# Phases of small matmuls placed next to each other in an attention kernel

## The chip, the core and the metric

The kernel runs on one core of one Trainium2 chip. The core has TensorE (PE in the profile; its weight loads are PEld), VectorE (DVE), ScalarE (ACT), GpSimd (POOL) and SyncE (SP), whose queue issues most DMAs. The metric is the device time of one execution in microseconds: 3090.34 us is the median of three runs (3089.7 to 3090.7).

## What is computed

The input is 8 images of 16 channels and 56 x 56 pixels. A convolution with nine 9 x 9 filters turns each image into 160 channels a pixel. Then come two transformer blocks with attention inside windows of 7 x 7 pixels, five heads of 32; the second block shifts the windows by three pixels and masks. A linear layer, a convolution back and a 1 x 1 convolution end it. Each block is:

```python
x = _ln(x, ln1g, ln1b)                       # over the 160 channels
qkv = _win_part(x) @ qkvw + qkvb
q, k, v = heads(...)                         # 49 positions, 5 heads, 32 wide
attn = softmax(q @ k.T * HEAD_DIM ** (-0.5) + bias (+ mask))
x = sc + _win_rev(attn @ v) @ projw + projb
x = x + gelu(_ln(x, ln2g, ln2b) @ w1 + b1) @ w2 + b2
```

## The kernel before

Three parts run one after the other: `phase_a` (first convolution and preparation of the weights, to about 170 us), `phase_b` (both blocks, to about 2890 us) and `phase_c` (the closing convolutions). The change is in `phase_b`.

`phase_b` works on strips of 14 rows of one image, 32 strips a layer, 64 in all. A function `body(i, la, lm, ln)` is written once for each engine, and `bodies` calls it for i from -1 to 64. A call mixes three strips: the attention of strip i (layer `la`), the MLP of strip i - 1 (layer `lm`), and the front part of strip i + 1 (layer `ln`: first norm, its turned copies, the products Q, K, V and B, where B holds the fifth head). Calls 1 to 32 have `lm` = 0, calls 33 to 63 have `lm` = 1; calls 2 to 30 and 34 to 62 run in loops. In this text a strip is one call of `body`, and it belongs to layer 0 or layer 1 by its `lm`. The MLP of layer 1 has one output tile more between the turn of z1 and Q0 (`mlp_out(2)`) and ends in four products `linear` with the closing linear layer.

The order of work on each engine is the order of the calls in its `body`; engines wait for each other on semaphores only. A wait holds all that stands behind it on its engine.

The attention of a strip has four groups of windows, j = 0 to 3. For each:

- `scores(j)` on TensorE writes q k into the first 245 columns of both PSUM banks of `so` (L1489); 20 products of 64 x 49, recorded as 40 matmuls. They wait for `s_sadd` (VectorE has read the scores before) and for `s_od` (VectorE has read earlier outputs), then comes a `nop`.
- `scores_biased(j)` on VectorE adds the bias into `sc` (L1248) and raises `s_sadd`; `scores_less_max(j)` takes the maximum (L1255) and subtracts it (L1258); `exps(j)` on ScalarE (L1089).
- `weights_turned(j)` on TensorE transposes the weights into `pt_ps` (L1498), `weights_out(j)` on ScalarE copies them to `pt` (L1094).
- `outputs(j)` on TensorE multiplies them by v into the columns from 256 of the same banks of `so` (L1510), again 40 recorded matmuls. `outputs(j)` on VectorE divides by the sum: a reciprocal (L1265) and two products into `os_` (L1268, L1272); it raises `s_od`.
- `outputs_turned(j)` on TensorE transposes `os_` (L1522); `outputs_hi(j)` on ScalarE (L1101) and `outputs_lo(j)` on VectorE (L1297) take it out in two parts.

Both kinds of small matmul use two row groups and two column groups of the array at once; row group r writes bank r of `so`. TensorE writes `so` only while VectorE does not read it, since both halves lie in the same banks.

Around them: `front_turned(hf)` on TensorE transposes z1 (L1430), which GpSimd completes (`repeat_rest`, L987); `front_hi(hf)` on ScalarE (L1053) and `front_lo(hf)` on VectorE (two operations, L1231) take it out; `front_product("Q", 0)` waits until the second operation of `front_lo(1)` is done. At the end of a strip `projection(n)` feeds the residual on VectorE (L1386), the statistics (L1182 to L1201), GpSimd's power (L1029), the second norm (L1205) and GpSimd's repeat of z2 (L987); then `mlp_turned(i, 0)` transposes z2 (L1430), and the next call's first `mlp_in` follows. `linear_out` on VectorE (L1286) takes out the linear products.

The time is set around the change by these lines on TensorE:

```python
reach(pe, s_od, n * NG + {0: 0, 1: 0, 2: 0, 3: 1}[j])      # scores(j, n), L1478
pe.wait_ge(s_sadd, i * NG + (3 if j == 0 else 4))           # outputs(j), L1504
if use == "Q0":
    pe.wait_ge(*a_freed(i, "T1C1"))                         # front_lo(1) is done
```

Of the kernel before, what the change touches and what calls it, by code (L numbers as in the profile page):

```python
# [45 lines left out]
NG = W // (2 * WIN)  # L46
# [660 lines left out]
def phase_b(nc, keep, late, xs0, xs1, ys):  # L707
    with ExitStack() as ctx:
# [333 lines left out]
        def _(act):  # L1042
            act_ = nc.scalar.activation

            def body(i, la, lm, ln):
# [91 lines left out]
                if la is not None:  # L1137
                    weights_out(0)
                    exps(2)
                if ln is not None:  # L1140
                    front_hi(1)
                if la is not None:
                    weights_out(1)
                    outputs_hi(0)
                if ln is not None:
                    queries(0)
                if la is not None:
                    weights_out(2)
                if ln is not None:
                    keys(0)  # L1150
                if la is not None:
                    outputs_hi(1)
                    exps(3)
# [23 lines left out]
        def _(dve):  # L1177
# [43 lines left out]
            def body(i, la, lm, ln):  # L1221
# [39 lines left out]
                def outputs(j):  # L1261

                    n = i * NG + j + 1
                    dve.wait_ge(s_of, n)
                    v.reciprocal(view(rd, 0, QP, 0, [[HEADS, 2], [1, HEADS]]),  # L1265
                                 view(so, 0, QP, OC + HD, [[512, 2], [VW, HEADS]])).then_inc(s_rec, 1)
# [81 lines left out]
                if lm is not None:  # L1348
                    mlp_out(0)
                if la is not None:  # L1350
                    scores_biased(2, i, la)
                    scores_less_max(2, i)
                if ln is not None:
# [3 lines left out]
                if la is not None:  # L1357
                    outputs(0)
                if ln is not None:
                    front_lo(1)  # L1360
                if lm == 1:
                    mlp_out(2)
                if la is not None:
                    scores_biased(3, i, la)
                    outputs_lo(0)
                    outputs(1)
                    scores_less_max(3, i)
                    outputs_lo(1)
                    outputs(2)
                    outputs(3)  # L1370
                    outputs_lo(2)
# [48 lines left out]
        def _(pe):  # L1420
# [12 lines left out]
            def body(i, la, lm, ln):  # L1433
# [38 lines left out]
                def scores(j, n):  # L1472
# [4 lines left out]
                    reach(pe, s_sadd, n * NG + j)  # L1477
                    reach(pe, s_od, n * NG + {0: 0, 1: 0, 2: 0, 3: 1}[j])  # L1478
                    pe.nop(nofuse=True)
# [21 lines left out]
                def outputs(j):  # L1501
                    pe.wait_ge(s_pte, i * NG + j + 1)
                    pe.wait_ge(*a_freed(i - 1, f"V{j}"))
                    pe.wait_ge(s_sadd, i * NG + (3 if j == 0 else 4))  # L1504
                    reach(pe, s_od, i * NG + j)
# [79 lines left out]
                if lm is not None:  # L1585
                    mlp_out(0)
                if la is not None:
                    scores(2, i)
                if ln is not None:
# [5 lines left out]
                if la is not None:  # L1595
                    outputs(0)
                if ln is not None:
                    front_turned(1)
# [6 lines left out]
                if la is not None:  # L1605
                    outputs_turned(0)
                    scores(3, i)
                if ln is not None:
                    front_product("Q", 0)
                if la is not None:  # L1610
                    outputs(1)
                    weights_turned(2)
                if ln is not None:
                    front_product("K", 0)
                if la is not None:
                    outputs_turned(1)
                if ln is not None:
# [13 lines left out]
                if la is not None:  # L1631
                    outputs(3)
                if lm is not None:
                    mlp_out(2 + lm)
# [14 lines left out]
                if ln is not None:  # L1649
                    values(2)  # L1650
                    scores(0, i + 1)
                if lm == 0:
# [321 lines left out]
```

## Time and profile before

| | |
|---|---|
| median of three runs | 3090.34 us |
| the profiled execution, first to last instruction | 3089.1 us |
| TensorE busy | 2989.3 us, 97% |
| weight loads busy | 2698.0 us, 87% |
| VectorE busy | 2223.4 us, 72% |
| ScalarE busy | 1715.3 us, 56% |
| GpSimd busy | 827.8 us, 27% |
| one strip, layer 0 / layer 1 | 40.86 / 44.37 us |

How to read the rows: times are microseconds from the start of the span. In a timeline a row is one instruction or several alike merged (x40), with its start, the time to the end of the last, the engine, the line of the kernel, and what is written from what. Brackets at the end hold the idle time of the engine before it and what ended it; "issue" means that nothing in the profile shows as the releaser. The ends of matmuls are modelled and overlap the next start, so the time between starts is what counts. A wait row gives the waiting engine, its tile and line, what it waited for, total, number of times and longest. In the list of windows, PEclk is the granted clock of TensorE as a share of its full 2.4 GHz.

### The profile page before, as it was taken

How to read it: one execution, taken by the hardware profiler on the slowest of the kernel's cores; microseconds unless marked ns; L12 is line 12 of the kernel's file. 1: busy time of each engine (PE TensorE's matmuls, PEld its weight loads, DVE VectorE, ACT ScalarE, POOL GpSimd, SP SyncE). 2: the span in 40 equal slices, each digit the busy share in tenths (PEclk: the TensorE clock that was granted, in tenths of full speed). 3: DMA queues.
4: the chain of work that ended last, by engine and by line, in shares of the span. 5: the costliest groups of instructions: out<-in, count | busy, mean ns of one | idle time of the engine just before them, and what ended most of it. 6: DMA issues, size and time to landing. Idle time of an engine off the chain costs nothing. (4 is left out here: it accounts for less than half of the span.)

```text
span 3089.1 us, 102841 instructions
## 1 busy us (share of the span) xinstructions
PE 2989.3 (97%) x39898; PEld 2698.0 (87%) x39898; DVE 2223.4 (72%) x6736; ACT 1715.3 (56%) x4076; POOL 827.8 (27%) x1470
## 2 busy tenths in 40 slices
PE   8889999999999999999999999999999999999799
PEld 6679888898888888898888888888888889888699
DVE  5667777777777777777777777777777777777422
ACT  6456656666655656666555655565556555655321
POOL 8122222222222222222232233223322332232110
PEclk9989999999999999999999999999999999999899
DMA  6411111111111111113111111111111111112284
GB/s 142 155 60 41 38 34 39 30 35 39 39 39 39 39 33 39 31 34 93 44 39 29 33 40 33 29 37 40 33 26 40 40 33 26 40 40 42 43 141 82
DMA packets 210425, 147.29 MB, mean 48 GB/s; under 512 B 15955, under 2 KB 205206, under 8 KB 210332
## 3 DMA queue, kind: packets, MB, share of 16 engines
q1 hardware_dynamic: 207619, 142.41, 19.7%
q10 hardware_dynamic: 1008, 3.44, 0.5%
q0 software_dynamic: 1728, 0.48, 0.1%
q8 instruction: 48, 0.79, 0.1%
q14 instruction: 22, 0.17, 0.0%
HBM read 95.64 MB, written 52.50 MB: 48 GB/s over the span
## 5 line engine op out<-in xcount | busy, mean ns | idle before, releaser
L1543 PE MATMUL rm<-w,ht 128*112 128x160 f32 x4480 | 682.7, 302 | 0.0
L1543 PEld LDWEIGHTS rm<-w,ht 128*112 128x112 f32 x4480 | 611.8, 177 | 5.2
L1029 POOL TENSOR_TENSOR rs<-ln_tmp,mhalf 112x4 f32<-112x4 f32 (+1 forms) x128 | 119.1, 931 | 1625.0 <-DVE ln_tmp L1201 1624.9
L1119 ACT ACTIVATE ht<-rm 128x448 f32<-128x448 f32 (+1 forms) x640 | 319.0, 498 | 193.4 <-PE rm L127 193.4
L1084 ACT ACTIVATE vb<-ra 113x320 f32<-113x320 f32 x256 | 113.1, 442 | 278.4 <-PE ra L127 276.8
L127 PE MATMUL rm<-z2t_hi,w_hi 128*128 128x448 f32 (+1 forms) x640 | 257.2, 402 | 4.4 <-DVE z2t_rest L1309 3.3
L987 POOL TENSOR_TENSOR z<-z,one 112x448 f32<-112x448 f32 (+2 forms) x192 | 131.3, 684 | 354.9 <-DVE z L1205 354.9
L127 PE MATMUL rm<-z2t_rest,w_rest 98*128 98x448 f32 (+1 forms) x640 | 219.9, 344 | 0.0
L127 PE MATMUL rm<-z2t_lo,w_hi 128*128 128x448 f32 (+1 forms) x640 | 219.1, 342 | 0.0
L127 PE MATMUL rm<-z2t_hi,w_lo 128*128 128x448 f32 (+1 forms) x640 | 218.2, 341 | 0.0
L1248 DVE TENSOR_TENSOR sc<-so,tabs 113x490 f32<-113x490 f32 x256 | 171.3, 669 | 54.8 <-PE so L1489 42.5
L1510 PEld LDWEIGHTS so<-vb,pt 49*49 49x49 f32 x10240 | 142.6, 122 | 60.3 <-issue 55.0
L1265 DVE RECIPROCAL rd<-so 113x10 f32<-113x10 f32 x256 | 56.1, 219 | 190.7 <-PE so L1510 183.0
L1101 ACT ACTIVATE ot_hi<-ra 128x98 fp32r<-128x98 f32 x512 | 103.1, 260 | 152.5 <-PE ra L1522 151.0
L127 PEld LDWEIGHTS rm<-z2t_hi,w_hi 128*128 128x128 f32 x640 | 121.0, 189 | 73.5 <-ACT ht L1119 37.1
L1258 DVE TENSOR_TENSOR sm<-sc,mx 113x490 f32<-113x490 f32 x256 | 173.1, 676 | 13.9
L1489 PEld LDWEIGHTS so<-kt,qm 64*49 64x49 f32 x8192 | 140.9, 122 | 48.0 <-issue 42.6
L1430 PE MATMUL ra<-ident,z 112*128 112x112 f32 (+1 forms) x1280 | 164.3, 268 | 14.8 <-POOL z L987 13.8
L1060 ACT ACTIVATE qm<-ra,qpair 128x400 f32<-128x400 f32 x256 | 138.2, 591 | 69.9 <-PE ra L127 69.9
L1255 DVE TENSOR_REDUCE mx<-sc 113x10 f32<-113x490 f32 x256 | 169.2, 661 | 6.4
L1489 PE MATMUL so<-kt,qm 64*49 64x49 f32 x8192 | 172.7, 208 | 1.0 <-ACT k L1076 1.0
L1510 PE MATMUL so<-vb,pt 49*49 49x33 f32 x10240 | 170.0, 210 | 2.9 <-issue 0.9
(258 smaller groups left out, 8848.5 us busy)
## 6 DMA issues: line engine op xcount, KB each, us to landing
xa<-xs SPq DMA_DIRECT2D x128, 245.0 KB
xr<-xs SPq DMA_DIRECT2D x128, 245.0 KB
xs<-xo SPq DMA_DIRECT2D x64, 245.0 KB
ys<-yz SPq DMA_DIRECT2D x64, 245.0 KB
c_y<-ys SPq DMA_DIRECT2D x36, 260.0 KB
xs<-a_tok SPq DMA_DIRECT2D x14, 560.0 KB, 6.6
xs<-tok_late SPq DMA_DIRECT2D x14, 560.0 KB, 6.8
a_nat<-in_x ACTq DMA_DIRECT2D x7, 480.0 KB, 6.4
```

What stands on the lines that cost most here:

```text
L127: last = nc.tensor.matmul(out, lhs, rhs, start=(n == 0), stop=(n == len(pairs) - 1))
L987: gp.tensor_tensor(view(t, 0, TT, t0 * ZW + DIM, [[ZW, nt], [REST, 2], [1, REST]]), once, view(one, 0, TT, 0, [[0, nt], [0, 2], [0, REST]] ...
L1029: gp.tensor_tensor(rs[1][:, t0:t0 + nt], ln_tmp[1][5][:, t0:t0 + nt], mhalf[:, 0:nt], ALU.pow).then_inc(s_pow, 1)
L1060: last = act_(qm[:, odd * QN + hf * QH:odd * QN + (hf + 1) * QH], bank_a(i, use)[:, 0:QH], ACT.Copy, scale=keep.qpair[:, odd:odd + 1])
L1119: act_(ht[:, f * SN + t0 * TT:f * SN + (t0 + nt) * TT], bank_m(i, lm, use)[:, 0:nt * TT], ACT.Gelu_apprx_tanh).then_inc(m_freed(i, lm, use ...
L1248: v.tensor_tensor(view(sc, 0, QP, 0, [[SX, 2], [1, SX]]), view(so, 0, QP, 0, [[512, 2], [1, SX]]), tab, ALU.add).then_inc(s_sadd, 1)
L1255: v.tensor_reduce(mx[:], s3, AX.X, ALU.max).then_inc(s_smax, 1)
L1258: v.tensor_tensor(sm[j % 2][:].rearrange("q (g k) -> q g k", k=WT), s3, view(mx, 0, QP, 0, [[1, 2 * HEADS], [0, WT]]), ALU.subtract).then_ ...
L1430: last = tr(bank_of(use)[0:rows, t * TT:(t + 1) * TT], z[:, c:c + rows], keep.ident[0:TT, 0:TT])
L1489: last = mm(so[w * WP:w * WP + WT, row * 512 + b * WT:row * 512 + (b + 1) * WT], q, k, start=True, stop=True)
L1510: last = mm(so[w * WP:w * WP + WT, p * 512 + OC + h * VW:p * 512 + OC + (h + 1) * VW], pt[p * WP:p * WP + WT, h * GK + w * WT:h * GK + (w ...
L1543: last = mm(bank_m(i, lm, use)[0:TT, t * DIM:(t + 1) * DIM], ht[:, c:c + TT], keep.w["w2", lm][:, f * DIM:(f + 1) * DIM], start=(f == 0), ...
```

## The change

On TensorE `scores(2)` goes from behind `mlp_out(0)` to right behind `outputs(0)`; `scores(3)` from before the product Q0 to right behind `outputs(1)`, which comes after Q0; the next strip's `scores(0)` from behind `values(2)` to right behind `outputs(3)`; `weights_turned(2)` from before K0 to behind it. The waits follow: outputs 0 and 1 wait only until the scores two groups back have been read (`min(j + 2, NG)`), and the next strip's scores 0 no longer wait for the outputs 3 to be read.

On VectorE, `outputs(j)` waits for `s_sfull`, that is until the scores behind the outputs are written as well: for j = 0 and 1 scores j + 2, for j = 3 the next strip's scores 0. `scores_biased(2)` goes behind `outputs(0)` and ahead of `front_lo(1)`, `scores_less_max(2)` behind that and the third MLP tile, `scores_biased(3)` behind `outputs(1)`. On ScalarE `exps(2)` goes behind `outputs_hi(0)`, and `keys(0)` ahead of `weights_out(2)`. No computation is added or left out.

```diff
--- before.py
+++ after.py
@@ -1136,19 +1136,17 @@
                     front_hi(0)
                 if la is not None:
                     weights_out(0)
-                    exps(2)
                 if ln is not None:
                     front_hi(1)
                 if la is not None:
                     weights_out(1)
                     outputs_hi(0)
+                    exps(2)
                 if ln is not None:
                     queries(0)
+                    keys(0)
                 if la is not None:
                     weights_out(2)
-                if ln is not None:
-                    keys(0)
-                if la is not None:
                     outputs_hi(1)
                     exps(3)
                 if ln is not None:
@@ -1262,6 +1260,10 @@
 
                     n = i * NG + j + 1
                     dve.wait_ge(s_of, n)
+                    if j < 2:
+                        dve.wait_ge(s_sfull, n + 2)
+                    if j == 3 and ln is not None:
+                        dve.wait_ge(s_sfull, n + 1)
                     v.reciprocal(view(rd, 0, QP, 0, [[HEADS, 2], [1, HEADS]]),
                                  view(so, 0, QP, OC + HD, [[512, 2], [VW, HEADS]])).then_inc(s_rec, 1)
                     dve.wait_ge(s_rec, n)
@@ -1347,23 +1349,22 @@
                     clear_rest()
                 if lm is not None:
                     mlp_out(0)
-                if la is not None:
-                    scores_biased(2, i, la)
-                    scores_less_max(2, i)
                 if ln is not None:
                     front_lo(0)
                 if lm is not None:
                     mlp_out(1)
                 if la is not None:
                     outputs(0)
+                    scores_biased(2, i, la)
                 if ln is not None:
                     front_lo(1)
                 if lm == 1:
                     mlp_out(2)
                 if la is not None:
-                    scores_biased(3, i, la)
+                    scores_less_max(2, i)
                     outputs_lo(0)
                     outputs(1)
+                    scores_biased(3, i, la)
                     scores_less_max(3, i)
                     outputs_lo(1)
                     outputs(2)
@@ -1475,7 +1476,7 @@
                         for name in "QKB":
                             pe.wait_ge(*a_freed(n - 1, f"{name}{j // 2}"))
                     reach(pe, s_sadd, n * NG + j)
-                    reach(pe, s_od, n * NG + {0: 0, 1: 0, 2: 0, 3: 1}[j])
+                    reach(pe, s_od, n * NG + {0: -1, 1: 0, 2: 0, 3: 1}[j])
                     pe.nop(nofuse=True)
                     for b in range(HEADS):
                         for row in range(2):
@@ -1501,7 +1502,7 @@
                 def outputs(j):
                     pe.wait_ge(s_pte, i * NG + j + 1)
                     pe.wait_ge(*a_freed(i - 1, f"V{j}"))
-                    pe.wait_ge(s_sadd, i * NG + (3 if j == 0 else 4))
+                    pe.wait_ge(s_sadd, i * NG + min(j + 2, NG))
                     reach(pe, s_od, i * NG + j)
                     pe.nop(nofuse=True)
                     for h in range(HEADS):
@@ -1584,8 +1585,6 @@
                     mlp_in(range(FT, 2 * FT))
                 if lm is not None:
                     mlp_out(0)
-                if la is not None:
-                    scores(2, i)
                 if ln is not None:
                     front_turned(0)
                 if la is not None:
@@ -1594,6 +1593,7 @@
                     mlp_out(1)
                 if la is not None:
                     outputs(0)
+                    scores(2, i)
                 if ln is not None:
                     front_turned(1)
                 if lm is None and la is None:
@@ -1604,15 +1604,15 @@
                     mlp_out(2)
                 if la is not None:
                     outputs_turned(0)
+                if ln is not None:
+                    front_product("Q", 0)
+                if la is not None:
+                    outputs(1)
                     scores(3, i)
                 if ln is not None:
-                    front_product("Q", 0)
-                if la is not None:
-                    outputs(1)
+                    front_product("K", 0)
+                if la is not None:
                     weights_turned(2)
-                if ln is not None:
-                    front_product("K", 0)
-                if la is not None:
                     outputs_turned(1)
                 if ln is not None:
                     front_product("B", 0)
@@ -1630,6 +1630,8 @@
                     values(1)
                 if la is not None:
                     outputs(3)
+                    if ln is not None:
+                        scores(0, i + 1)
                 if lm is not None:
                     mlp_out(2 + lm)
                 if la is not None:
@@ -1648,7 +1650,8 @@
                     mlp_out(4 + lm)
                 if ln is not None:
                     values(2)
-                    scores(0, i + 1)
+                    if la is None:
+                        scores(0, i + 1)
                 if lm == 0:
                     mlp_out(5)
                 if lm == 1:
```

## Rows read from the trace of the kernel before

**Rows 1.** Windows over one strip of each layer: us, busy by engine, granted clock.
```profile
core 0: us, PE busy (x) PEld busy (x) DVE busy (x) ACT busy (x) POOL busy (x), PEclk, DMA share, GB/s
1041.86:1082.72 40.86, 40.69 (x585) 36.56 (x579) 31.40 (x100) 24.88 (x62) 10.80 (x22) 1.00 0.14 37
1991.30:2035.67 44.37, 43.50 (x607) 39.48 (x606) 33.64 (x107) 24.89 (x64) 11.91 (x19) 1.00 0.14 35
```

**Rows 2.** Timeline, layer 0, scores 3 and Q0: start, us, engine, line, operation.
```profile
635.05 0.25 PE L1489 MATMUL so<-kt,qm 64*49 64x49 f32 x2
635.52 0.21 PE L1489 MATMUL so<-kt,qm 64*49 64x49 f32 x2
635.66 0.45 PE L127 MATMUL ra<-z1t_hi,qkv_hi 128*128 128x400 f32 x1
```

**Rows 3.** Waits of the weight loads, 300 to 1500 us: total, times, longest.
```profile
PEld so L1489 <- issue: 19.2, 89, 0.3
```

**Rows 4.** Timeline, same strip, what leads to outputs 0, all engines.
```profile
628.22 0.93 POOL L987 TENSOR_TENSOR z<-z,one 112x448 f32<-112x448 f32 x1 [2.12 <-DVE z L1205]
629.09 1.13 ACT L1089 ACTIVATE pr<-sm 113x490 f32<-113x490 f32 x2
629.86 0.98 PE L1430 MATMUL ra<-ident,z 112*128 112x112 f32 x8
630.50 0.59 ACT L1053 ACTIVATE z1t_hi<-ra 128x448 fp32r<-128x448 f32 x1 [0.28 <-PE ra L1430]
631.43 0.56 ACT L1094 ACTIVATE pt<-pt_ps 113x490 f32<-113x490 f32 x1
632.62 0.66 PE L1510 MATMUL so<-vb,pt 49*49 49x33 f32 x40
633.22 0.80 PE L1430 MATMUL ra<-ident,z 112*128 112x112 f32 x6
```

**Rows 5.** Timeline, same strip, VectorE from outputs 0 to scores 3.
```profile
633.53 0.21 DVE L1265 RECIPROCAL rd<-so 113x10 f32<-113x10 f32 x1
634.38 0.50 DVE L1231 TENSOR_TENSOR z1t_lo<-ra,z1t_hi 128x336 fp32r<-128x336 f32 x1
634.91 0.50 DVE L1231 TENSOR_TENSOR z1t_rest<-ra,z1t_rest 32x336 fp32r<-32x336 f32 x1
635.80 0.67 DVE L1248 TENSOR_TENSOR sc<-so,tabs 113x490 f32<-113x490 f32 x1 [0.39 <-PE so L1489]
```

**Rows 6.** Timeline, same strip, its last part.
```profile
644.47 0.22 DVE L1265 RECIPROCAL rd<-so 113x10 f32<-113x10 f32 x1 [2.82 <-PE so L1510]
650.04 0.66 DVE L1386 TENSOR_TENSOR x<-ra,xr 112x480 f32<-112x480 f32 x1 [0.86 <-PE ra L127]
653.27 0.25 PE L1489 MATMUL so<-kt,qm 64*49 64x49 f32 x2
654.88 0.61 POOL L987 TENSOR_TENSOR z<-z,one 112x256 f32<-112x256 f32 x1 [1.29 <-DVE z L1205]
655.62 0.77 PEld L1430 LDWEIGHTS rm<-ident,z 112*128 112x128 f32 x8 [0.39 <-issue]
```

**Rows 7.** Waits in layer 1, 1600 to 2800 us.
```profile
PE rm L127 <- DVE yz L1286: 12.0, 27, 0.4
PEld rm L1430 <- DVE yz L1286: 14.4, 27, 0.5
```

**Rows 8.** Timeline, a strip of layer 1, from z1 to Q0.
```profile
2062.88 0.93 POOL L987 TENSOR_TENSOR z<-z,one 112x448 f32<-112x448 f32 x1 [3.40 <-DVE z L1205]
2068.62 0.21 DVE L1265 RECIPROCAL rd<-so 113x10 f32<-113x10 f32 x1
2070.00 0.50 DVE L1231 TENSOR_TENSOR z1t_rest<-ra,z1t_rest 32x336 fp32r<-32x336 f32 x1
2071.87 0.45 PE L127 MATMUL ra<-z1t_hi,qkv_hi 128*128 128x400 f32 x1
```

**Rows 9.** Timeline and window at the seam of the layers.
```profile
1518.34 0.48 PE L127 MATMUL rm<-z2t_hi,w_hi 128*128 128x448 f32 x1 [1.99 <-DVE z2t_rest L1309]
1519.50:1523.00 3.50, 3.50 (x15) 3.09 (x13) 2.06 (x8) 2.12 (x5) 3.34 (x9) 0.51 0.26 68
```

More of the change, by code:

```diff
@@ L1606, in body @@
                     outputs_turned(0)
-                    scores(3, i)
                 if ln is not None:
@@ L1611, in body @@
                     outputs(1)
-                    weights_turned(2)
+                    scores(3, i)
                 if ln is not None:
@@ L1615, in body @@
                 if la is not None:
+                    weights_turned(2)
                     outputs_turned(1)
```

## The prediction

> **What bounds the kernel now.** I read the busy times by stretch first, then who waited for whom, then the instructions in order of time, for one strip of each layer. The strips are alike to 0.01 us, so one stands for all of its layer. A strip of layer 0 takes 40.86 us and TensorE is busy in 40.69 of them; one of layer 1 takes 44.37 us with 43.50 busy [rows 1]. That looks like a TensorE bound, in which every 0.3 us that is taken off a strip shows in the time. The other rows say that this holds in the first part of a strip alone.
>
> A phase of small matmuls, here scores 3, shows what is to be won: 40 recorded matmuls start within 0.47 us (635.05 to 635.52), yet Q0 starts only at 635.66, 0.61 us after the phase began [rows 2]. Ahead of such a phase the weight loads stand idle for 19.2/89 = 0.22 us [rows 3]. So a phase alone takes about 0.22 + 0.61 = 0.83 us, of which 0.48 are its matmuls and 0.35 its two edges.
>
> In a strip of layer 0, TensorE's order around the change is turn z1 (first half), transpose of weights 0, mlp_out 1, outputs 0, turn z1 (second half), transpose of weights 1, transpose of outputs 0, scores 3, Q0. What Q0 needs besides TensorE is the last half of `front_lo` on VectorE, which ends at 634.91 + 0.50 = 635.41; Q0 starts at 635.66 [rows 2, 5]. Q0 is thus only 0.19 us short of waiting for VectorE, and it is scores 3 that fills the time.
>
> At the end of the strip TensorE waits already. From the residual (650.04, which waits 0.86 us for the projection) a chain runs over VectorE's statistics, GpSimd's power, the normalisation and GpSimd's repeat of z2, which ends at 654.88 + 0.61 = 655.49; the turn of z2 starts at 655.62, after 0.39 us of idle weight loads. Scores 0 of the next strip (from 653.27, 0.6 us) and mlp_out 5 behind it are what TensorE does under that chain [rows 6]. In layer 1 the same place shows 12.0 us over 27 strips before the third linear product and 14.4 us before the turn, both for VectorE's yz [rows 7]: 0.44 and 0.53 us a strip. There too the chain starts at the projection.
>
> **The change part by part.** *The three seams.* Each of three phases per strip loses its edges and keeps its 0.48 us of matmuls, plus what the seam itself costs. No row shows two such phases back to back. From below it is 0, since no matmul goes away; from above it is 0.22 us, the idle time at entering one from other work [rows 3], if the waits and the nop ahead of the second phase empty the engine. I take c = 0.05, nearer to 0: the semaphores named there were all raised long before. The Trainium skill, TensorEngine Tiling (Array Packing), Key Properties, says that it is a change of the tiling mode that drains the engine, not a change of tile. By that c is 0 and the sum below comes to 3122 us; by the row's upper end it comes to 3163. The row cannot tell the mode from the wait.
>
> *Scores 2 behind outputs 0, layer 0.* Scores 2 took 0.60 us and its entry ahead of the turn of z1 at 629.86, so TensorE could now start that turn at about 629.1, but GpSimd's repeat of z1 ends at 628.22 + 0.93 = 629.15 [rows 4]: 629.21 instead of 629.86. Outputs 0 came 2.76 us after that turn [rows 4], and follows at 629.21 + 2.73 = 631.94. ScalarE lets it: the two exponentials end at 629.09 + 1.13 = 630.22, the eviction of the turn and of weights 0 then takes as long as before (630.50 to 631.43 + 0.56, so 1.49), 631.71 [rows 4]. Scores 2 starts at 631.94 + 0.48 + c = 632.42 + c.
>
> VectorE now waits at outputs 0 for scores 2 as well, and the wait stands in order ahead of everything behind it. It used to follow a start of scores 3 by 635.80 - 635.05 = 0.75 us [rows 2, 5], so the reciprocal begins at 633.17 + c instead of 633.53, 0.36 us earlier less c. But `scores_biased(2)`, 0.67 us with 0.03 to the next, now stands between it and `front_lo(1)`: that one moves by -0.36 + c + 0.70 = +0.34 + c, to 635.75 + c, and with 0.06 us to TensorE Q0 starts at 635.81 + c. TensorE would be ready for it at 634.5: turn, weights 1 and outputs 0 turned took 1.83 us from the turn's start to scores 3 (633.22, 0.60 after outputs 0, to 635.05). It stands for some 1.2 us. Q0 comes 0.15 + c later than before, and scores 3 has not been run yet.
>
> *Scores 3 behind outputs 1, layer 0.* It now comes after Q0: 0.48 + c, and 0.01 as edge. This is a cost, since the gap that it filled is still there. Behind it, `exps(2)` comes at about 637.2 on ScalarE and is over before K0 has ended; I followed ScalarE's row of queries, keys, weights, fifth head and values and found nothing late for TensorE by more than 0.1 us in layer 0.
>
> *Scores 0 behind outputs 3, both layers.* It adds 0.49 + c ahead of the projection. From there on the chain sets the end of the strip; taking 0.6 to 0.8 us of matmuls out from under it only turns them into idle time, so nothing comes back. VectorE's wait at outputs 3 is covered: it stood idle for 2.82 us before that step [rows 6].
>
> *Sum, layer 0:* 0.15 + 0.49 + 0.49 + 3c = 1.13 + 3c = 1.28 us a strip, for 32 strips 41 us.
>
> *Layer 1.* The repeat of z1 is there early (2062.88 + 0.93 = 2063.81), so all begins 0.65 rather than 0.6 us sooner, and the reciprocal, at 2068.62 before, moves by about -0.44 + c. `front_lo(1)` ended at 2070.50; it moves by +0.26 + c, Q0 to 2070.82 + c instead of 2071.87 [rows 8]. The third tile of mlp_out, some 1.4 us of TensorE between the turn and Q0, now covers the wait, and TensorE itself arrives at the same time. That is a gain of 1.05 us; scores 3 takes 0.49 + c of it and scores 0 another 0.49 + c: -0.07 + 3c = +0.08 us, with up to 0.2 for ScalarE being late, and 0.05 back at outputs 1, which need not wait for scores 3 to be read. Times 30 strips: 2 us. The last strip, without a front, gains about 1 us.
>
> *Total:* 41 + 2 - 1 = 42 us on the profiled execution (span 3089.1 us; the median of the runs, 3090.3, is 1.2 above it): 3132.
>
> **Rivals.**
> A. *As summed:* 3132. With c from 0 to 0.22 it is 32 x 1.13 - 3 - 1 = +32 to 32 x 1.79 + 30 x 0.6 - 2 = +73, 3122 to 3163. For it: every link is a row, and strips repeat exactly.
> B. *Faster: TensorE alone sets the pace.* Then 191 seams return 0.35 - c = 0.30 each, 57 us: 3033. It asks that Q0 doesn't wait for `front_lo(1)` and that the end of the strip isn't a chain. It decides where VectorE reaches the end of `front_lo(1)` before 634.5 in layer 0, over 1.2 us sooner than summed. Against it: outputs 0 alone takes 0.85 us there (633.53 to 634.38) and the two halves of `front_lo` 1.03 [rows 5].
> C. *Only one of the two is right*, for example the move of scores 0 comes back because TensorE's earlier arrival starts the chain's links sooner: 62 x 0.49 = 30 us less, 3102. Against it: the 0.39 us wait before the turn of z2 [rows 6], and the 0.44 and 0.53 of layer 1 [rows 7].
> D. *The clock falls.* The new waits are some 1.2 us twice in a strip. After one of 1.99 us, at the seam of the layers, the granted clock was 0.51 for 3.5 us, the lower level of 1.2 GHz [rows 9]: at most half of it, 1.7 us, is lost. In the strips with waits of 0.4 to 0.5 us it stayed at 1.00 [rows 1]. If it fell in every second strip: 31 x 1.7 = 53 us more, 3185; in one of four, 3158. The Trainium skill, TensorE: Matmul & The Clock Gate, on HAM oscillation, describes a loop in which pauses bring the clock down again and again; no row of this case has such a loop.
> E. *The seam saves nothing:* each second phase drains as if entered afresh. Then c is 0.3, the upper end and more: 32 x 2.03 + 30 x 0.85 - 2 = +88, 3178.
>
> **How the numbers follow.** A 0.60, B 0.08, C 0.11, D 0.14, E 0.07. The time is that of A, 3132. The range for 8 in 10 takes in A whole, the upper half of C, D for up to about every third strip: 3105 to 3170. A measurement of this kernel can tell 0.2%, 6 us, from no change. Faster: B, 0.08. Same: the lower part of C, 0.05. Slower: the rest, 0.87.
>
> **What would show it.** In the changed kernel's timeline of layer 0, Q0 has about 1.2 us of idle TensorE before it, ended by VectorE's `front_lo` (z1t_rest); before the turn of z2 the idle weight loads grow from 0.39 to some 1.1 us; in layer 1 the wait for yz before the third linear product grows from 0.44 to about 1.2. The strips take 42.1 and 44.4 us. Scores 2 starts about 0.5 us after outputs 0. I am wrong if layer 0 strips are below 41 us, if Q0 waits for nothing, or if the wait before the turn of z2 stays at 0.4. A granted clock below 1.00 in the middle of a layer is D.

## The result

The changed kernel takes 3214.4 us (median of 4 runs, 3211.9 to 3215.9) against 3090.5 us for the kernel before in the same runs: ratio 1.0396, 95% interval 1.0381 to 1.0411, so 4.0% slower. The forecast was 3132 us, with 3105 to 3170 as its range: the sign was right, the size was not. The profiled execution has a span of 3210.4 us. One of the four executions of the version with the third seam alone (below) took 5326 us at a lower granted clock, 0.859 over the span; its time is given as the median of the other three.

TensorE's part of the page after the change, busy time, share of the span and count:

```profile
span 3210.4 us, 102974 instructions
PE 3025.4 (94%) x39898; PEld 2753.4 (86%) x39898; DVE 2217.5 (69%) x6736; ACT 1701.0 (53%) x4076; POOL 832.2 (26%) x1470
```

The work is the same to the instruction (39898), and its busy time has grown by only 36 us of the 121 us by which the span grew. The rest is idle. The windows over a strip of layer 0 and two of layer 1 answer to [rows 1]; columns as there, the granted clock being the third number from the end:

```profile
970.66:1013.24 42.58, 40.52 (x581) 36.53 (x580) 31.33 (x100) 24.58 (x62) 10.91 (x23) 1.00 0.14 35
2402.10:2447.05 44.95, 43.05 (x608) 39.41 (x608) 33.51 (x108) 24.65 (x62) 12.46 (x19) 1.00 0.15 34
2588.03:2635.49 47.46, 45.70 (x609) 42.20 (x608) 33.52 (x108) 24.82 (x62) 11.94 (x20) 0.93 0.14 32
```

Layer 0 takes 42.59 us a strip (42.58 in this window) instead of 40.86; the 29 strips from 247 to 1482 us agree to 0.03 us. Layer 1 comes in two kinds: 44.95 us at a clock of 1.00, as in the second line (before: 44.37), and up to 47.7 us with a clock of 0.93 over the strip, as in the third. Of the 28 strips from 1610 to 2913 us, 7 are of the first kind, 14 take 47.3 to 47.7 us, and 7 lie between, at 46.2 to 46.3 us.

The middle of a strip of layer 0, timeline of TensorE and VectorE, answers to [rows 2, 4, 5]:

```profile
991.00 0.66 PE L1511 MATMUL so<-vb,pt 49*49 49x33 f32 x40
991.72 0.25 PE L1490 MATMUL so<-kt,qm 64*49 64x49 f32 x2
992.46 0.22 DVE L1267 RECIPROCAL rd<-so 113x10 f32<-113x10 f32 x1 [1.04 <-PE so L1490]
993.32 0.66 DVE L1246 TENSOR_TENSOR sc<-so,tabs 113x490 f32<-113x490 f32 x1
993.89 0.50 DVE L1229 TENSOR_TENSOR z1t_lo<-ra,z1t_hi 128x336 fp32r<-128x336 f32 x1
994.42 0.50 DVE L1229 TENSOR_TENSOR z1t_rest<-ra,z1t_rest 32x336 fp32r<-32x336 f32 x1
995.05 0.45 PE L127 MATMUL ra<-z1t_hi,qkv_hi 128*128 128x400 f32 x1 [0.99 <-DVE z1t_rest L1229]
996.00 0.66 PE L1511 MATMUL so<-vb,pt 49*49 49x33 f32 x40
996.48 0.23 PE L1490 MATMUL so<-kt,qm 64*49 64x49 f32 x2
```

Scores 2 starts 0.72 us after outputs 0, scores 3 0.48 us after outputs 1. VectorE stands idle 1.04 us and begins the outputs at 992.46, when scores 2 is written; bias 2 (993.32) stands before the two parts of `front_lo(1)` (993.89, 994.42), and TensorE waits 0.99 us for the second of them before Q0. Before the change Q0 had no idle time in front of it.

Its end answers to [rows 6]:

```profile
1003.65 0.66 PE L1511 MATMUL so<-vb,pt 49*49 49x33 f32 x40
1004.38 0.25 PE L1490 MATMUL so<-kt,qm 64*49 64x49 f32 x2
1010.70 0.66 DVE L1387 TENSOR_TENSOR x<-ra,xr 112x480 f32<-112x480 f32 x1 [0.85 <-PE ra L127]
1015.54 0.61 POOL L987 TENSOR_TENSOR z<-z,one 112x256 f32<-112x256 f32 x1 [1.30 <-DVE z L1203]
1016.28 0.98 PE L1431 MATMUL rm<-ident,z 112*128 112x112 f32 x8 [0.90 <-POOL z L987]
1016.28 0.76 PEld L1431 LDWEIGHTS rm<-ident,z 112*128 112x128 f32 x8 [1.15 <-issue]
```

Scores 0 follow outputs 3 after 0.73 us. From the residual to the turn of z2 it is 1016.28 - 1010.70 = 5.58 us, as before (655.62 - 650.04 = 5.58): the chain has not moved at all, and the idle time of the weight loads in front of the turn has grown from 0.39 to 1.15 us (0.90 us for the matmuls, which had none before).

The end of a strip of layer 1 with the low clock, timeline of TensorE and the windows that follow; it answers to [rows 7, 9]:

```profile
2591.58 0.33 PE L127 MATMUL rm<-lin_hi,z2t_hi 128*112 128x160 f32 x1 [1.21 <-DVE yz L1288]
2593.37 1.75 PE L1431 MATMUL rm<-ident,z 112*128 112x112 f32 x8 [0.27 <-DVE yz L1288]
2592.80:2599.60 6.80, 6.53 (x28) 5.81 (x28) 6.05 (x24) 2.49 (x4) 4.01 (x5) 0.50 0.58 137
2599.60:2610.00 10.40, 10.40 (x101) 9.31 (x100) 6.31 (x15) 8.14 (x18) 4.54 (x12) 1.00 0.06 9
```

The wait for yz before the third linear product is 1.21 us instead of 0.44. Then the granted clock is 0.50, the lower of its two levels, for 6.8 us, and the turn of z2 takes 1.75 us instead of 0.98.

The same waits stand in the strips of layer 1 that keep the full clock. In the strip from 2402.10 us (44.95 us, clock 1.00, above) they are 1.21 and 0.37 us, and at the seam of the layers, where the clock fell before the change [rows 9], a wait of 1.85 us is followed by no fall:

```profile
1573.69 0.47 PE L127 MATMUL rm<-z2t_hi,w_hi 128*128 128x448 f32 x1 [1.85 <-DVE z2t_rest L1311]
1570.00:1610.00 40.00, 38.15 (x565) 34.90 (x563) 29.91 (x87) 24.15 (x61) 10.33 (x17) 1.00 0.18 45
2405.65 0.33 PE L127 MATMUL rm<-lin_hi,z2t_hi 128*112 128x160 f32 x1 [1.21 <-DVE yz L1288]
2407.43 0.79 PE L1431 MATMUL rm<-ident,z 112*128 112x112 f32 x6 [0.37 <-DVE yz L1288]
```

### The profile page after: what moved, and what is told of

It reads as the page before. It is cut to its first block and busy times, and to the rows that moved or that the text cites. A ratio compares the mean times of both kernels' runs of the same rounds, so it can differ in the third digit from the quotient of the medians.

```text
span 3210.4 us, 102974 instructions
## 1 busy us (share of the span) xinstructions
PE 3025.4 (94%) x39898; PEld 2753.4 (86%) x39898; DVE 2217.5 (69%) x6736; ACT 1701.0 (53%) x4076; POOL 832.2 (26%) x1470
## 5 line engine op out<-in xcount | busy, mean ns | idle before, releaser
L1029 POOL TENSOR_TENSOR rs<-ln_tmp,mhalf 112x4 f32<-112x4 f32 (+1 forms) x128 | 119.3, 932 | 1697.6 <-DVE ln_tmp L1199 1697.5
L1089 ACT ACTIVATE pr<-sm 113x490 f32<-113x490 f32 x256 | 152.2, 619 | 101.5 <-DVE sm L1256 100.7
L127 PE MATMUL ra<-z1t_hi,qkv_hi 128*128 128x400 f32 (+1 forms) x384 | 168.7, 439 | 32.9 <-DVE z1t_rest L1229 32.7
```

The costliest lines, as they stand in the source:

```text
L127: last = nc.tensor.matmul(out, lhs, rhs, start=(n == 0), stop=(n == len(pairs) - 1))
L1089: act_(view(pr[j % 2], 0, QP, 0, [[WP, 2 * HEADS], [1, WT]]), view(sm[j % 2], 0, QP, 0, [[WT, 2 * HEADS], [1, WT]]), ACT.Exp).then_inc(s_e ...
```

## The experiments

What the theories are. Theory 1: from the projection on, the end of a strip is a chain, so that moving scores 0 ahead of the projection is cost alone. Theory 2: a seam costs what the waits written at it cost. Theory 3 (with 3b and 3c): in layer 0 VectorE's order of work sets Q0 and what follows. Theory 4: the clock falls because of the longer idle time at the end of the strips of layer 1. Times of strips are distances between GpSimd's first power (L1029) of one strip and that of the next.

**Two seams only.** From the changed kernel:

```diff
                     outputs(3)
-                    if ln is not None:
-                        scores(0, i + 1)
...
                     values(2)
-                    if la is None:
-                        scores(0, i + 1)
+                    scores(0, i + 1)
...
-                    if j == 3 and ln is not None:
-                        dve.wait_ge(s_sfull, n + 1)
...
```

TensorE's scores 0 wait again for the reading of outputs 3, as before the change.

> The changed kernel with the next strip's scores 0 back in their old place (behind values 2), and VectorE's wait for them at outputs 3 gone; seams 0+2 and 1+3 stay. Theory 1 (the end of a strip is a chain from the projection, so scores 0 ahead of the projection are pure cost, 0.48 us plus a seam of 0.25): 0.73 us less a strip than the changed kernel, layer 0 at 41.9 us, layer 1 at 44.2, and with the old short waits at the end the granted clock stays 1.00 in layer 1; about 3117 us. Rival (TensorE sets the pace, and something else made the change slow): the strips stay as in the changed kernel or get longer by the edges of a phase, 0.35 us; the clock still falls.

Measured: 3118.1 us, ratio 1.0086 (1.0069 to 1.0103). Windows over a strip of each layer:

```profile
1000.96:1042.80 41.84, 40.62 (x581) 36.56 (x580) 31.46 (x100) 24.59 (x62) 10.94 (x23) 1.00 0.15 36
2074.00:2118.17 44.17, 43.14 (x609) 39.47 (x608) 33.51 (x108) 24.66 (x62) 12.46 (x20) 1.00 0.15 35
```

41.84 us and 44.18 us, clock 1.00. The two seams cost 0.98 us a strip in layer 0 and give back 0.19 in layer 1. Without the third seam the clock doesn't fall.

**The third seam only.** From the kernel before, the same edit the other way round: `scores(0, i + 1)` behind `outputs(3)`, and VectorE's wait there; scores 0 no longer wait for the reading of outputs 3.

> The kernel before with the third seam alone: the next strip's scores 0 right behind outputs 3, and VectorE's wait there. Theory 1: 0.73 us more in every strip, layer 0 at 41.6 us, layer 1 at 45.1, the wait before the turn of z2 in layer 0 grows from 0.39 to over 1 us; 3136 us if the clock stays, up to 3188 if the longer waits at the end of layer 1's strips are what makes it fall. Rival: an edge is saved, 0.3 us less a strip, 3070 us.

Measured: 3212.2 us, ratio 1.0393 (1.0366 to 1.042): this seam alone is as slow as the whole change, though its layer 0 is about 31 us shorter. Windows over a strip of each layer:

```profile
995.13:1036.76 41.63, 40.62 (x580) 36.55 (x580) 31.29 (x100) 24.86 (x62) 10.80 (x22) 1.00 0.14 36
2100.17:2147.95 47.78, 46.07 (x608) 42.36 (x608) 33.57 (x108) 25.02 (x62) 11.89 (x19) 0.93 0.14 32
```

Layer 0 takes 41.63 us, 0.77 more than before. In layer 1 the strips of 45.1 us that were expected occur once (45.11); nearly all take 47.6 to 47.8 us, at a clock of 0.93. The upper of the two expected totals was 3188; the fall of the clock costs more than that allowed for.

**The waits ahead of the outputs.** From the changed kernel:

```diff
+                def products_read(j, n):
+                    for name in "QKB":
+                        pe.wait_ge(*a_freed(n - 1, f"{name}{j // 2}"))
...
+                    products_read(2, i)
                     outputs(0)
-                    scores(2, i)
+                    scores(2, i, True)
...
+                    if ln is not None:
+                        products_read(0, i + 1)
                     outputs(3)
                     if ln is not None:
-                        scores(0, i + 1)
+                        scores(0, i + 1, True)
```

> The changed kernel, but the three waits of scores 2 and of scores 0 for ScalarE's reads of Q, K and B stand ahead of the outputs before them instead of at the seam. They are raised long before either way. Theory 2 (a seam costs what the waits written at it cost: 0.24 us with five waits at scores 2 and 0, 0.00 us with two at scores 3): both seams go to 0.00, layer 0 strips to 42.1 us, layer 1's undisturbed ones to 44.5, about 30 us less than the changed kernel, 3184. Rival (the seam is the array's or the bank's, scores 3 differ by something else): seams stay at 0.24 and the time at 3214.

Measured: 3205.2 us (3186.6 to 3206.1 over 5 runs), ratio 1.0367 (1.0349 to 1.0384); the profiled execution, 3186.6 us, is the shortest of them, and in it the clock stays at 1.00 from the seam of the layers until 1916 us, so the strips say more than the total. TensorE's timeline, outputs 0 with scores 2 and outputs 3 with scores 0:

```profile
1025.45 0.66 PE L1514 MATMUL so<-vb,pt 49*49 49x33 f32 x40
1025.92 0.23 PE L1493 MATMUL so<-kt,qm 64*49 64x49 f32 x2
1037.83 0.66 PE L1514 MATMUL so<-vb,pt 49*49 49x33 f32 x40
1038.45 0.25 PE L1493 MATMUL so<-kt,qm 64*49 64x49 f32 x2
```

The first seam goes from 0.72 to 0.47 us, which is no cost, the second from 0.73 to 0.62. Layer 0 takes 42.20 us instead of 42.59, an undisturbed strip of layer 1 44.51 instead of 44.95. Theory 2 holds for three quarters of what it was asked: 0.36 of 0.49 us. At scores 0, where the same two waits are left as at scores 3, 0.14 us stay; what they are is open.

**`front_lo` first.** From the changed kernel, VectorE:

```diff
                 if la is not None:
                     outputs(0)
-                    scores_biased(2, i, la)
                 if ln is not None:
                     front_lo(1)
+                if la is not None:
+                    scores_biased(2, i, la)
```

> The changed kernel, but on VectorE front_lo(1) stands ahead of scores_biased(2) instead of behind it. Theory 3 (Q0 in layer 0 waits for VectorE's order: outputs 0, bias 2, front_lo): Q0 comes 0.55 us sooner (bounded by ScalarE's eviction of the turn), the idle time before it falls from 0.99 to about 0.45, layer 0 at 42.0 us, layer 1 hardly moved; about 3196 us. Rival (the wait before Q0 is covered by a later one): strips stay at 42.6, 3214 us.

Measured: 3216.1 us, ratio 1.0402 (1.0385 to 1.0419): nothing gained, layer 0 at 42.60 us. TensorE's timeline in layer 0, Q0 and the turn of outputs 1 (weight load and matmul):

```profile
1037.30 0.45 PE L127 MATMUL ra<-z1t_hi,qkv_hi 128*128 128x400 f32 x1 [0.51 <-DVE z1t_rest L1229]
1041.08 0.38 PEld L1524 LDWEIGHTS ra<-ident,os 113*128 113x128 f32 x4 [0.46 <-DVE os L1274]
1041.08 0.60 PE L1524 MATMUL ra<-ident,os 113*128 113x113 f32 x4 [0.26 <-DVE os L1274]
```

The wait before Q0 fell from 0.99 to 0.51 us, as expected, and a new one stands before the turn of outputs 1, on VectorE's outputs 1. Theory 3 as it stood, that Q0's wait is the cost, falls.

**No maximum of scores 2.** VectorE, from the changed kernel and from the kernel before; the maximum of scores 2 is left out of the computation, which only shortens VectorE's work (here and in the run that follows it):

```diff
-                    v.tensor_reduce(mx[:], s3, AX.X, ALU.max).then_inc(s_smax, 1)
+                    if j != 2:
+                        v.tensor_reduce(mx[:], s3, AX.X, ALU.max).then_inc(s_smax, 1)
...
```

> The changed kernel without the row maximum of scores 2 on VectorE (0.66 us a strip; the subtraction takes the maximum of scores 1, so the softmax of group 2 is shifted by another amount). Theory 3b (in layer 0 VectorE's row of work from outputs 0 to outputs 2 is the bound, the wait before Q0 being only the first place where it shows): layer 0 falls by about 0.6 us a strip, to 42.0, layer 1 by some of it; 3190. Rival (TensorE sets the pace behind Q0): layer 0 stays at 42.6 us, 3214.

> The kernel before without the row maximum of scores 2 on VectorE, as counterpart of the last one. Theory 3b: before the change VectorE was not the bound there, so nothing moves: 40.86 and 44.37 us a strip, 3090. Rival (VectorE bound the middle of the strip already before the change): some 0.3 to 0.6 us less in each strip of layer 0, 3075.

Measured, from the changed kernel: 3213.8 us, ratio 1.0387 (1.0371 to 1.0404), layer 0 at 42.60 us. The waits of TensorE between 300 and 1500 us there:

```profile
PE ra L127 <- DVE z1t_rest L1229: 27.8, 28, 1.0
```

Q0 waits 27.8/28 = 0.99 us as in the changed kernel, since the maximum lies behind `front_lo`. From the kernel before: 3080.0 us, ratio 0.9971 (0.9957 to 0.9985), layer 0 at 40.69 us instead of 40.86, layer 1 unmoved. VectorE was thus late by 0.17 us a strip in layer 0 already before the change; I had taken that to be nothing.

**Both.** The two edits on the changed kernel together.

> The changed kernel with both earlier edits: front_lo(1) ahead of scores_biased(2), and no row maximum of scores 2 on VectorE (the subtraction takes that of scores 1). Each alone left layer 0 at 42.60 us. Theory 3c (two rows of VectorE's work end equally late there: front_lo before Q0, and bias 2, maximum 2, outputs 1 before the turn of outputs 1; one alone only hands the wait to the other): layer 0 falls by about 0.5 us, to 42.1; about 3198 us with the clock of layer 1 as in the changed kernel. Rival (neither bounds it, the strip is set by the end of the strip alone): 42.6 us again, 3214.

Measured: 3197.4 us, ratio 1.0353 (1.0336 to 1.0369), layer 0 at 42.12 us, 0.48 less. The waits of TensorE between 300 and 1500 us:

```profile
PE ra L127 <- DVE z1t_rest L1229: 14.5, 29, 0.5
```

Each edit alone gives 0.0, both give 0.48: two rows of VectorE's work end at the same time there, `front_lo` before Q0, and bias, maximum, subtraction and outputs 1 before the turn of outputs 1. What bounds layer 0 behind outputs 0 is VectorE, which has been held idle for 1.04 us and then has the bias, 0.57 us from its start to the next operation, more to do before `front_lo`. This is theory 3c. Part of the 0.48 need not be the change's: the shorter work of VectorE gave 0.17 in the kernel before as well.

**Idle products against the fall of the clock.** From the changed kernel, layer 1 only:

```diff
                 if lm == 1:
-                    linear(range(4))
+                    linear(range(2))
+                    for _ in range(4):
+                        mm(pt_ps[0:TT, 0:DIM], keep.ident[:, 0:TT], keep.w["w2", lm][:, 0:DIM], start=True, stop=True)
+                    linear(range(2, 4))
```

> The changed kernel with four idle products (128 x 112 by 160 columns, into pt_ps, which nobody reads then) between the second and the third linear product of layer 1, where TensorE waits some 1.2 us for VectorE's yz. Nothing is left out of the result. Theory 4 (the clock falls because of the idle time at the end of the strips of layer 1, and costs what is lost beyond the undisturbed strip of 44.95 us): the added work fits into the wait, the granted clock stays at 1.00, all strips of layer 1 take 44.95 us, the whole about 55 us less than the changed kernel, 3160. Rival (the clock falls for the sum of idle time over a strip, or because of what stands before Q0): the clock keeps falling, 3214 or more.

Measured: 3166.0 us, ratio 1.0239 (1.0223 to 1.0255). Timeline of TensorE at the end of a strip of layer 1 (the four products are recorded as eight matmuls), and the window over the middle of layer 1:

```profile
2021.70 1.27 PE L1660 MATMUL pt_ps<-w,ident 128*112 128x160 f32 x8
2024.85 0.98 PE L1431 MATMUL rm<-ident,z 112*128 112x112 f32 x8 [0.38 <-DVE yz L1288]
1700.00:2700.00 1000.00, 982.48 (x13608) 900.62 (x13608) 746.12 (x2394) 545.30 (x1368) 278.17 (x423) 1.00 0.15 34
```

The products fill the wait for yz, which is no longer there; the granted clock is 1.00 from 1700 to 2700 us, and every strip there takes 44.9 to 45.0 us. With more work on TensorE the kernel is 48 us faster than the changed one. Theory 4 holds.

**The same on the third seam alone.**

> The kernel before with the third seam alone, and in layer 1 the four idle products in TensorE's wait before the third linear product. Theories 1 and 4: without a fall of the clock the third seam alone costs 0.77 us a strip in layer 0 and 0.74 in layer 1; strips of 41.63 and 45.1 us, clock 1.00, about 3138 us against 3216 without the idle products. Rival (the third seam alone keeps a second reason for the fall): above 3190.

Measured: 3138.7 us, ratio 1.0153 (1.0137 to 1.017). Windows over a strip of each layer and over the middle of layer 1:

```profile
996.10:1037.70 41.60, 40.58 (x580) 36.50 (x580) 31.24 (x100) 24.88 (x62) 10.93 (x22) 1.00 0.14 36
2079.39:2124.52 45.13, 44.53 (x616) 40.47 (x616) 33.60 (x108) 24.88 (x62) 12.45 (x19) 1.00 0.15 34
1700.00:2700.00 1000.00, 986.39 (x13667) 896.49 (x13666) 744.51 (x2372) 553.40 (x1383) 273.68 (x418) 1.00 0.15 34
```

41.60 and 45.13 us, clock 1.00. So the third seam costs 0.75 us a strip by itself, 47 us, and by the clock another 74 us.

**The seams where they pay.** Layer 0 as before the change; in layer 1 the first two seams, with the waits for Q, K and B ahead of outputs 0. The diff shows the two new places on TensorE; the old ones are left to layer 0. VectorE and ScalarE have the order of the changed kernel in layer 1, but for the third seam.

```diff
                 if la is not None:
+                    if lm == 1:
+                        products_read(2, i)
                     outputs(0)
+                    if lm == 1:
+                        scores(2, i, True)
...
                     outputs(1)
...
+                    if lm == 1:
+                        scores(3, i)
...
```

> The kernel before in layer 0; in layer 1 the seams 0+2 and 1+3 with ScalarE's and VectorE's order of the changed kernel, the three waits for Q, K and B ahead of outputs 0, and scores 0 where they were before. Theories 1 and 2: layer 0 strips at 40.86 us, layer 1 at 44.19 (as in the run with two seams) less 0.24 for the seam, 43.95, clock 1.00; 0.42 us times 30 less than before, about 3078, 0.4% faster. Rival (in layer 1 VectorE is as late as in layer 0, so an earlier seam gives nothing): 44.19 us, 3085.

Measured: 3075.2 us, ratio 0.9945 (0.9932 to 0.9959). Windows over a strip of each layer:

```profile
979.09:1019.95 40.86, 40.69 (x580) 36.58 (x580) 31.36 (x100) 24.87 (x62) 10.91 (x23) 1.00 0.14 37
2037.99:2081.85 43.86, 42.94 (x608) 39.37 (x608) 33.50 (x108) 24.64 (x62) 12.44 (x19) 1.00 0.16 35
```

40.86 and 43.86 us: 0.51 us less in layer 1, 0.09 more than expected.

**The opposite of the third seam.** V1, 8 matmuls, from before outputs 3 to behind the projection:

```diff
-                if ln is not None:
+                if ln is not None and la is None:
                     values(1)
                 if la is not None:
                     outputs(3)
...
                 if ln is not None:
+                    if la is not None:
+                        values(1)
                     values(2)
                     scores(0, i + 1)
...
```

ScalarE's copies of V1 and its place in the ring of banks move with it.

> The kernel before with that move of V1 alone. Theory 1: layer 0 40.5 us, layer 1 44.37 less 0.8, 43.6; about 3054 us. Rival: 3090.

> The last version (seams in layer 1 only, 3075 us) with the product V1 (8 matmuls, 0.9 us of TensorE) moved from before outputs 3 to behind the projection, and its place in the ring of banks with it: the opposite of what the third seam does. Theory 1 (from the projection on the strip's end is a chain that leaves TensorE waiting): the strips get shorter by what TensorE waits there, 0.39 us in layer 0 and about 0.8 in layer 1, 40.5 and 43.1 us, together 36 us: 3039. Rival (the waits at the end only move, since every engine there is near its bound): 3075 or more.

Measured, on the kernel before: 3072.9 us, ratio 0.994 (0.9925 to 0.9956), strips of 40.56 and 44.03 us. On the version with the seams in layer 1: 3070.4 us, ratio 0.9943 (0.9929 to 0.9958), strips of 40.55 and 44.01 us. Waits in layer 1 of the former, 1600 to 2800 us:

```profile
PEld rm L127 <- DVE yz L1288: 6.4, 27, 0.2
PEld rm L1432 <- DVE yz L1288: 14.4, 27, 0.5
```

In layer 0 the strip loses 0.30 us, close to the 0.39 that TensorE waited. In layer 1 it loses 0.34 instead of 0.8. The wait of the weight loads before the third linear product fell to 6.4/27 = 0.24 us, from 0.60 in the kernel before (16.2/27 over the same stretch), but the one before the turn of z2 stayed at 14.4/27 = 0.53 us [rows 7]. I had added the two as if both were room; the second is not shortened by work that is moved ahead of the third product. Together with the seams V1's move makes layer 1 longer, 44.01 against 43.86; why was not looked into. The two versions and the one above can't be told apart by their times, and all three beat the kernel before by 0.5 to 0.6%, and with it the changed one.

## Why the prediction was right in sign and wrong in size

Of the 124 us by which the kernel got slower the forecast had 42. The mechanism that it named is there: Q0 waits for VectorE's z1t_rest (0.99 us, 1.2 forecast), the weight loads stand idle 1.15 us before the turn of z2 (1.1 forecast), and TensorE waits 1.21 us for yz in layer 1 (1.2 forecast). So the sign was not luck. What failed are two terms: the cost of the seams, and the fall of the clock, which the sum had at nothing.

*What TensorE's edges are worth.* Right for one seam of three: scores 3 behind outputs 1 begins after 0.48 us, so that a seam can be free.

*The seam's own cost c.* Mis-sized. I took 0.05 for each; they measured 0.24, 0.00 and 0.25. The step that failed is "the semaphores named there were all raised long before": between two phases of only 0.48 us, waits that were met long before still cost. Scores 2 and 0 have three waits more than scores 3, and moving those away took 0.36 of the 0.49 us; for the rest no run shows a cause. In the sum this is 32 x (0.49 - 0.15) + 30 x (0.49 - 0.15) = 21 us.

*Scores 2 behind outputs 0, layer 0.* Right in place and size. From one strip's power to the next one's Q0 it was 23.95 us before (635.66 - 611.71) and is 24.39 after (995.05 - 970.66): 0.44 later, where 0.15 + 0.24 = 0.39 was the sum with the measured c. Part of the fit is luck: VectorE began outputs 0 only 0.02 us sooner in the strip (633.53 - 611.71 = 21.82 us after the power before, 992.46 - 970.66 = 21.80 after), where 0.36 less c is 0.12, and the bias delayed what stands behind it by 0.57 us (993.32 to 993.89) and not 0.70. The reason that I gave was incomplete: I held the wait before Q0 to be the only one, and two rows of VectorE's work end there together.

*Scores 3 and scores 0, layer 0.* Right: 0.49 + 0.00 + 0.49 + 0.25 = 1.23 against 1.27 measured from Q0 to the next power (16.92 before, 18.19 after). Layer 0 in all: 1.62 worked out with the measured c, 1.73 measured, 55 us over 32 strips; the forecast had 41.

*Layer 1.* Forecast +0.08 us a strip, with the measured c +0.42; undisturbed strips have +0.58, 17 us over 30. The third seam there is 0.75 of it, as forecast with its c (0.74); the first two give back 0.19. What fell short is the gain at Q0, taken at 1.05 less c, 0.81 with the measured c. It came at 27.36 us after the power before the change (2071.87 - 2044.51) and comes at 26.79 after it (2428.89 - 2402.10), 0.57 sooner:

```profile
2428.89 0.44 PE L127 MATMUL ra<-z1t_hi,qkv_hi 128*128 128x400 f32 x1
```

*The clock.* This is where most of the size was lost, and it was my rival D. The sum had it at nothing, and I gave D 0.14 and at most one strip in two. Filling the wait takes 3214.4 to 3166.0 us: 48 us. The step that failed is the comparison by length: I set the new waits against the one of 1.99 us at the seam of the layers [rows 9] and against those of 0.4 to 0.5 us, and took a fall in some of the strips as the worst case. The waits that the clock fell behind were 1.21 us long, and it did not fall behind one of 1.85. In layer 0, where TensorE waits 0.99 us before Q0 and 0.90 before the turn, the clock stays at 1.00; in layer 1, where the wait of 1.21 us before the third linear product is followed by one of 0.27 to 0.47 us before the turn of z2 (the places of [rows 7]), it falls in most strips. I had also capped a fall at 3.5 us of low clock and 1.7 us lost; here it lasts 6.8 us in half of the strips and costs up to 2.7.

*The sum, as measured:* 55 + 17 + 48 = 120 us of 124. Of the 82 us that the forecast lacks, 48 are the clock and 21 the seams; the other 13 are 4 in layer 0, 5 in layer 1, and 4 outside this sum.

*Rivals.* B, the faster case, fell with the waits before Q0 and before the turn of z2. C, that the third seam returns something, fell with the unchanged 5.58 us from residual to turn. E, that each second phase drains as if entered afresh, had nearly the size of c for two seams of three (0.3 against 0.24) and not the reason: scores 3 cost nothing, and 0.36 of the 0.49 us of the other two went with the waits.

## What to carry to other kernels

An engine that is busy 97% of the time may still be led by others in parts of a loop: a step moved out from under a wait saves nothing where it leaves and costs in full where it goes. Before you put two small phases together, count the waits between them and hoist those that are met anyway, and look whose work the second phase now stands ahead of. When a change lengthens a wait on TensorE, price the fall of the clock at the full length that a trace shows and in every turn of the loop; work that nobody needs, put into the wait, is the quickest way to see what the clock costs.

## What the runs showed of the hardware

Two tiled phases in a row cost 0.47 to 0.48 us from start to start at scores 3, and at scores 2 once three of its five waits stand ahead; this is the time of their 40 matmuls. It is 0.72 us with five waits at scores 2, and at scores 0 it is 0.73 with five and 0.62 with two. The Trainium skill, TensorEngine Tiling (Array Packing), Key Properties, has the engine drain at a change of the tiling mode and not at a change of tile; the 0.47 us agree with it.

The clock's fall repeats itself: with the third seam alone, nearly every strip of layer 1 had 6.8 us at the lower level and took 47.8 us, where the same strips with idle products in the wait kept 1.00 and took 45.1. Before each of these falls stood a wait of 1.2 us. The length of the wait does not decide by itself: waits of 1.21 and 0.37 us, and one of 1.85, left the clock at 1.00 in other places of the changed kernel, and before the change one of 1.99 us was followed by a fall [rows 9]. Two falls that follow each other in the changed kernel, and the stretch between them:

```profile
1705.30:1712.10 6.80, 6.78 (x33) 6.23 (x33) 4.87 (x21) 2.37 (x3) 3.36 (x5) 0.50 0.36 81
1712.15:1753.00 40.85, 39.35 (x579) 36.40 (x578) 28.82 (x89) 22.41 (x59) 8.80 (x16) 1.00 0.10 24
1753.10:1759.85 6.75, 6.73 (x32) 6.09 (x31) 5.18 (x22) 2.37 (x3) 3.64 (x5) 0.50 0.43 104
```

They begin 47.8 us apart, although the strips there take 47.4 us, so that the fall comes later in each strip than in the one before, 3.7 to 5.2 us after its power, until a strip comes with a fall of 3.4 us (46.2 us in all) and then two with none. With the third seam alone falls are 47.8 us apart too, and there a strip takes as long: the fall is met again in every turn. That fits the 74 us that the clock costs there and the 48 in the changed kernel. In layer 0, with one wait of 0.99 and one of 0.90 us in a strip, the clock did not fall. Which property of the waits decides was not separated.
